# First attention of a six-layer kernel: the causal mask leaves TensorE and is added by GpSimd, and three steps are put in another order

## The reference

```python
scores = jnp.einsum('bhqd,bhkd->bhqk', qh, kh) * inv_sqrt_d
causal = jnp.tril(jnp.ones((sq, sk), dtype=bool))
scores = jnp.where(causal, scores, jnp.finfo(scores.dtype).min)
attn = jax.nn.softmax(scores, axis=-1)
out = jnp.einsum('bhqk,bhkd->bhqd', attn, vh)
return out.transpose(0, 2, 1, 3).reshape(b, sq, H) @ Wout.T      # x = x + this
```

## Time and profile before

| | |
|---|---|
| median of 3 runs | 1257.46 us (1254.38 to 1261.32) |
| the profiled execution | 1256.03 us |
| its span | 1254.2 us |
| busy in the span | PE 91%, PEld 70%, DVE 57%, ACT 35%, POOL 21% |
| mean granted clock of TensorE | 0.96 |

### The profile page before, as it was taken

How to read it: one execution, slowest core, us unless ns; L and a number is a source line. 1 busy time by engine, 2 the same in 40 slices (tenths; PEclk the granted TensorE clock), 3 DMA queues, 4 the chain that set the end, 5 groups by cost and what they waited for, 6 DMA issues and landing times. The chain is left out here.

```text
span 1254.2 us, 32458 instructions
## 1 busy us (share of the span) xinstructions
PE 1141.8 (91%) x12589; PEld 872.6 (70%) x12590; DVE 720.3 (57%) x1834; ACT 443.3 (35%) x1283; POOL 267.3 (21%) x343
## 2 busy tenths in 40 slices
PE   3899899999999889999969999999984887889997
PEld 1676688787887668987957777777754775546664
DVE  3788554455455465553257878888763998212221
ACT  0444353443343211211046555555521332112221
POOL 1600000000000000000144456445415220322222
PEclk9999899999999989999689999999996997899999
DMA  7521000000000076000002111111148112122221
GB/s 234 180 58 45 1 1 1 0 0 0 0 0 1 1 197 156 0 0 9 27 10 54 48 32 51 51 42 35 44 153 277 37 32 80 40 60 38 43 39 14
DMA packets 69644, 65.54 MB, mean 52 GB/s; under 512 B 32720, under 2 KB 60656, under 8 KB 68940
## 3 DMA queue, kind: packets, MB, share of 16 engines
q1 hardware_dynamic: 61612, 45.32, 14.0%
q0 software_dynamic: 7968, 19.32, 5.2%
HBM read 52.34 MB, written 13.19 MB: 52 GB/s over the span
## 5 line engine op out<-in xcount | busy, mean ns | idle before, releaser
L1532 ACT ACTIVATE xattn_exps<-xattn_ps_s,xattn_top 128x256 f32<-128x256 f32 x256 | 118.0, 475 | 77.5 <-DVE xattn_top L1600 77.5
L613 PEld LDWEIGHTS attn_ps_q<-attn_xnT,w_b_q 128*128 128x128 f32 x1024 | 118.8, 193 | 12.6 <-issue 12.6
L613 PE MATMUL attn_ps_q<-attn_xnT,w_b_q 128*128 128x128 f32 x1024 | 123.4, 276 | 0.0
L1099 POOL TENSOR_TENSOR fold_last_cos<-raw_last,all_consts 64x64 f32<-64x64 f32 x1 | 0.3, 314 | 538.3 <-POOLq L911 538.3
L667 PE MATMUL attn_ps_out<-w_b_o,attn_oT 128*128 128x256 f32 x480 | 106.5, 380 | 1.8 <-DVE all_x L848 1.5
L667 PEld LDWEIGHTS attn_ps_out<-w_b_o,attn_oT 128*128 128x128 f32 x480 | 90.0, 190 | 15.1 <-DVE all_x L848 2.4
L1607 DVE STREAM_TRANSPOSE xattn_expsT<-xattn_exps 128x1024 f32<-128x1024 f32 x64 | 79.5, 1242 | 22.6 <-ACT xattn_exps L1532 22.6
L721 ACT COPY attn_qT<-attn_ps_q 128x512 f32<-128x512 f32 x64 | 38.0, 594 | 148.2 <-PE attn_ps_q L613 148.2
L1597 DVE TENSOR_REDUCE xattn_raw_top<-xattn_ps_s 128x4 f32<-128x1024 f32 x64 | 77.8, 1216 | 13.6 <-PE xattn_ps_s L1424 13.3
L1424 PE MATMUL xattn_ps_s<-xattn_kT,xattn_qT 64*32 64x256 f32 x2048 | 69.6, 381 | 2.9 <-ACT xattn_exps L1532 2.9
L1434 PE MATMUL xattn_ps_o<-xattn_expsT,xattn_kv 32*64 32x256 f32 x2048 | 63.5, 380 | 4.6 <-DVE xattn_last_scores L1643 3.9
(11 more groups left out here) (325 smaller groups left out, 2309.2 us busy)
## 6 DMA issues: line engine op xcount, KB each, us to landing
xattn_inverse<-xattn_inverse_rows SPq DMA_DIRECT2D x30, 256.0 KB, 4.1
all_c<-in_ctx SPq DMA_DIRECT2D x64, 64.0 KB, 1.9
moe_gate<-in_f_gate SPq DMA_DIRECT2D x8, 512.0 KB, 8.6
moe_up<-in_f_up POOLq DMA_DIRECT2D x8, 512.0 KB, 7.2
moe_down<-in_f_down POOLq DMA_DIRECT2D x8, 512.0 KB, 12.9
sorted_x<-all_zeros SPq DMA_DIRECT2D x1, 2944.0 KB, 15.7
experts_x_in<-sorted_x SPq DMA_DIRECT2D x23, 128.0 KB, 2.3
xattn_v_stage<-xattn_v_rows SPq DMA_DIRECT2D x16, 136.0 KB, 1.8
```

Of the source, the lines that this page charges most:

```text
L613: last = nc.tensor.matmul(ps_q[g % 2][:, h * P:(h + 1) * P], wq[:, c, head * DH:(head + 1) * DH], xnT[u][:, c, :], start=(c == 0), stop=(c ...
L1532: nc.scalar.activation(exps[g % 2][:, nkeys * k:nkeys * (k + 1)], ps_s[g % 2][:, nkeys * k:nkeys * (k + 1)], ACT.Exp, bias=top[u][:, n:n + ...
```

## The change

In the first layer alone (`cross`):

- The two mask products per tile (L320) are dropped; the score products start their own accumulation.
- VectorE turns the 32 columns of the mask table once at the start (`causalT`), ahead of the roots of the first normalisation. Per tile, after VectorE has turned the scores (L506), GpSimd adds the turned mask, broadcast over heads, to them (128x512, f32, both inputs in SBUF) and writes `masked`; VectorE takes the maximum and the difference from `masked`.
- On VectorE, `softmax_head` is split. In step i the order becomes outs_ready(i-2), normalise(i+2), turn the scores of i, queries_out(i+1), then `softmax_rest(i)` (wait for GpSimd, maximum, difference), residual(i-2).
- On TensorE, turn_exps(i-1) moves from behind scores(i) to behind queries(i+1), directly ahead of finish(i-2); turn(i+2) moves behind weigh(i-1) and behind the waits of scores(i+1). On ScalarE, expsT_out(i-1) moves behind the copies of keys and values.
- `load_and_scale` becomes a generator: its first part (the loads for the second layer) runs first, then two scale operations after each of the first tiles' mask adds, and the loads `c_1` and `c_2` after that of tile 9.

```diff
-            if beside:
+            if cross:
+                work = beside(pool)
+                causal = causalT[:, :].unsqueeze(1).to_broadcast([P, HEADS, SEQ])
+                pool.wait_ge(causal_turned, 1)
+                next(work)
+                for t in range(TILES):
+                    pool.wait_ge(scores_out, t + 1)
+                    wait_count(pool, shifted_ready, t)
+                    nc.gpsimd.tensor_tensor(masked[:, :, :], scores_sb[:, :].rearrange("p (h k) -> p h k", h=HEADS), causal, ALU.add)\
+                      .then_inc(masked_ready, 1)
+                    if t < BESIDE_STEPS:
+                        next(work)
+            else:
                 beside(pool)
...
-            def scores(t):
+            def scores_waits(t):
                 pe.wait_ge(q_ready, t + 1)
                 pe.wait_ge(k_ready, t + 1)
                 wait_count(pe, scores_out, t)
-                for p in range(2):
-                    nc.tensor.matmul(ps_scores[:, 512 * p:512 * p + 256], ident16, causal16, start=True, stop=False, skip_group_check=True)
+
+            def scores(t):
+                if not cross or isinstance(t, int):
+                    scores_waits(t)
+                if not cross:
+                    for p in range(2):
+                        nc.tensor.matmul(ps_scores[:, 512 * p:512 * p + 256], ident16, causal16, start=True, stop=False, skip_group_check=True)
...
             def step(i, u, live):
                 if live(0):
                     scores(i)
-                if live(-1):
+                if not cross and live(-1):
                     turn_exps(i - 1)
                 if cross and live(-2):
                     turn_outs(i - 2, i + 2 if live(1) else TILES)
                 if live(1):
                     keys_values(i + 1, 1 - u)
                     queries(i + 1, 1 - u)
+                if cross and live(-1):
+                    turn_exps(i - 1)
                 if cross and live(-2):
                     finish(i - 2, i if live(-1) else TILES)
-                if live(2):
+                if not cross and live(2):
                     turn(i + 2)
                 if live(-1):
                     weigh(i - 1, 1 - u)
+                if cross and live(2):
+                    if live(1) and live(0):
+                        scores_waits(i + 1)
+                    turn(i + 2)
...
             if cross:
+                nc.vector.transpose(causalT[:, :], consts[:, C_CAUSAL:C_CAUSAL + SEQ]).then_inc(causal_turned, 1)
                 moments.roots(dve, dve_roots, EPS_LN)
...
             def softmax_head(t):
                 dve.wait_ge(scores_made, t + 1)
+                if cross:
+                    wait_count(dve, masked_ready, t)
                 for p in range(2):
                     last = nc.vector.transpose(scores_sb[:, p * 256:(p + 1) * 256], ps_scores[:, 512 * p:512 * p + 256])
                 last.then_inc(scores_out, 1)
-                dve.wait_ge(scores_out, t + 1)
+
+            def softmax_rest(t):
+                if cross:
+                    dve.wait_ge(masked_ready, t + 1)
+                    view = masked[:, :, :]
+                else:
+                    dve.wait_ge(scores_out, t + 1)
+                    view = scores_sb[:, :].rearrange("p (h k) -> p h k", h=HEADS)
                 s1.tile(t)
-                view = scores_sb[:, :].rearrange("p (h k) -> p h k", h=HEADS)
...
                 if live(0):
                     softmax_head(i)
+                    if not cross:
+                        softmax_rest(i)
                 if live(1):
                     if not cross:
                         values_out(i + 1, 1 - u)
                     queries_out(i + 1)
+                if cross and live(0):
+                    softmax_rest(i)
                 if live(-2) and cross:
                     residual(i - 2)
```

More of the change, by code:

```diff
@@ L26 @@
 MASKED = -1e30
+BESIDE_STEPS = 10
 C_IDENT = 0
@@ L217, in small_attention @@
     shifted = sb("shifted", [P, HEADS, SEQ])
+    masked = sb("masked", [P, HEADS, SEQ]) if cross else None
+    causalT = sb("causalT", [P, SEQ]) if cross else None
+    masked_ready, causal_turned = sem("masked_ready"), sem("causal_turned")
     exps = sb("exps", [P, HEADS * SEQ])
@@ L260, in _ @@
                 nc.gpsimd.memset(v_rows[u][:, :, :, HD], 1.0).then_inc(blank, 1)
-            if beside:
+            if cross:
[11 more added lines that the diff above has]
+            else:
                 beside(pool)
-            if not cross:
                 for t in range(TILES):
@@ L326, in scores @@
                             last = nc.tensor.matmul(ps_scores[rows, 512 * p + m * P:512 * p + (m + 1) * P], kT[half, m, rows],
-                                                    q_blocks[half, m, :, rows], start=False, stop=True, skip_group_check=True)
+                                                    q_blocks[half, m, :, rows], start=cross, stop=True, skip_group_check=True)
                 last.then_inc(scores_made, 1)
@@ L440, in step @@
                         values_out(i + 1, 1 - u)
+                if cross and live(-1):
+                    expsT_out(i - 1)
                 if live(0):
@@ L2112, in load_and_scale @@
             pool.dma_start(c_br[:, :], d["c_br"].partition_broadcast(P)).then_inc(got_c, 16)
+            yield
             for c in range(KC):
@@ L2116, in load_and_scale @@
                       .then_inc(b_scaled, 1)
+                    if n // SCALED % 2:
+                        yield
                 nc.gpsimd.tensor_scalar(b_kv[:, c, :], b_kv[:, c, :], b_g[:, c:c + 1], None, ALU.mult).then_inc(b_scaled, 1)
+            yield
             pool.dma_start(c_1[:, :, :], chunks(d["c_w1"])).then_inc(got_c, 16)
             pool.dma_start(c_2[:, :, :], chunks(d["c_w2"])).then_inc(got_c, 16)
+            yield
         phase = ExitStack()
```

## The result

The changed kernel takes 1274.53 us in the median of 4 runs (1273.60 to 1276.49), the kernel before 1259.01 us (4 runs, 1254.38 to 1261.32). The ratio is 1.0106, with a 95% interval of 1.0083 to 1.0130: slower by about 13 us by this ratio (the two medians lie 15.5 us apart), where +12.0 was forecast. The forecast was 1268.5 us with a range of 1263 to 1275, so the median lies just inside its upper edge. The profiled execution after took 1273.60 us, its span 1271.8 us.

The account below looks back on a forecast made before the run. VectorE's own 5.2 us per tile was taken as the bound, giving way to a 6.34 us chain: 13 steps 82.4 against 71.99, +10.4; with 0.2, 1.25 and 0.15, +12.0, forecast 1268.5 us, range 1263 to 1275.

Parts of the forecast that it names:

- the chain through VectorE: First layer: maximum and difference lengthen the closed TensorE-VectorE chain from 5.00 to 6.34 us per step; chance 0.70.
- VectorE's list is the bound before, so the mask products are worth 0: First layer: VectorE alone needs 5.2 us per tile, so freeing 0.31 us of TensorE per tile gains nothing.
- TensorE's order: finish waits for ScalarE's copy, about 0.85 us idle per step; TensorE's sum 5.8 us, covered by the 6.34 us chain.
- The add hidden up to about 2.1 us: GpSimd's mask add, taken as 1.46 us, costs nothing in a steady step up to about 2.1 us.
- The tail and the start: Last tile's bare add +1.25 us; tile 0's outputs +0.2; the mask turn ahead of the roots +0.15.
- The loads: Third layer's loads move to tile 9; the values' stall, 4.4 us, is gone; colliding again +4.4, 1273, chance 0.08.
- TensorE as the bound: Rival: the chain doesn't close and TensorE gets shorter, step 4.9 us, whole 1249.3; chance 0.05.
- GpSimd over its limit: Rival: GpSimd's add over 2.1 us, or its scale operations holding up the difference, whole 1274; chance 0.08.
- The clock: Rival: TensorE's clock falls in the new gaps, in half of the steps, +13, whole 1281; chance 0.03.
- The port rule: Shared VectorE-GpSimd port: the difference would wait up to 0.9 us in some ten steps; half of a 0.08 chance.

Follow-up runs that it names:

- x11: Kernel before with its old orders, no causal mask at all, loads spread as in the change and TensorE's wait for queries ahead of weigh: ratio 0.9971 to the kernel before.
- x1: Changed kernel with TensorE's and ScalarE's order of before: ratio 1.0113 to the kernel before.
- x3: Changed kernel without GpSimd's add, so the mask is left out: ratio 1.0125 to the kernel before.
- x8: x7 with the projection also in the free half of a scores bank: ratio 1.0046 to the kernel before.
- x2: Changed kernel with the projection written to the free half of a scores bank, every order kept: ratio 1.0169 to the kernel before.
- x6: Kernel before (mask products, VectorE's order, no add) with only TensorE's and ScalarE's new order and the loads spread: ratio 1.0103 to the kernel before.
- x7: Changed kernel with VectorE's maximum and difference moved a step later, ScalarE's exponential moved to match: ratio 1.0142 to the kernel before.
- x4: Changed kernel with the mask added twice on GpSimd: ratio 1.0187 to the kernel before.
- x5: Changed kernel with VectorE's maximum and difference back ahead of the masking of the queries: ratio 1.0179 to the kernel before.

## Why the prediction was right

The time lay in the range for the reason given, the chain through VectorE. Of the 6.0 us between the forecast of 1268.5 and the median of 1274.53 the first layer accounts for 1.5 (13.5 instead of 12.0). The forecast also started from 1256.5 us for the kernel before, which took 1259.01 in the median of four, 2.5 more; the remaining 2.0 us lie within the scatter of the other layers.

*VectorE's list is the bound before, so the mask products are worth 0.* Right: L320 is gone and nothing was gained. In x11, where they are simply left out, the step is no shorter than before.

*The chain through VectorE, 6.34 us.* Right as a mechanism, shown by x1 and x3: without TensorE's order, and without the add, the step stays 6.40 us and VectorE waits ahead of the queries. x8 against x2 shows it from the other side. It was sized 0.06 us short, 0.8 in 13 steps. The turned outputs to the last query product took 79.63 + 1.16 - 78.62 = 2.17 us and not 2.12, and I had taken the shorter of the two lengths that the stretch from L482 to the end of L486 alternates between. The first five steps took 6.5 each, 0.1 more than the others, 0.5 in all. Together +11.75 and not +10.4.

*TensorE's order: "the wait is covered by the chain. If that cover went, TensorE would set 5.8".* This is the step of the prediction that failed. The wait itself was right (0.77 us), its price without cover was not. I added it to TensorE's own list, and did not follow what waits for the instruction behind it: the projection feeds the residual, and the residual stands ahead of the outputs in VectorE's queue. x6 measures 6.35 us where the prediction said 5.8 and the expectation 6.0. It did no harm to the forecast because the other chain is as long (6.40), and two chains of nearly equal length cost no more than one. That was luck: nothing in the prediction compared the two, and a second chain 0.1 us longer would have set the step. It would have misled anyone who mended only the first (x7).

*The add hidden up to about 2.1 us.* Right, if a little short: in x4 the two adds, 2.6 us with their handover, stuck out by 0.3, so the limit is near 2.3. The add took 1.27 us, not 1.46. GpSimd's groups after:

```profile
L273 POOL TENSOR_TENSOR xattn_masked<-xattn_scores,xattn_causalT 128x512 f32<-128x512 f32 x16 | 20.3, 1271 | 57.7 <-DVE xattn_scores L537 57.7
```

VectorE's subtraction on as many elements takes 0.69 us. The Trainium skill, "GPSIMD Engine Reference", section "4.1 Engine selection", has GpSimd about twice as slow for two inputs; here it is 1.84 times.

*The tail and the start.* The end part took +1.66 us against 1.25 forecast, with the bare wait of 1.38 us where it was expected (131.83); the start took +0.09 against 0.35.

*The loads.* TensorE waited for the values once, 0.8 us, instead of 4.2: no collision at tile 9. This single wait was not forecast. The 4.4 us that I took out hold for the one trace I had read: the collision cost 0.4 us in the second trace of before, and the two differ by 2.3 us over the same 13 steps.

*The rivals.* TensorE as the bound: excluded by x11 and by the gaps. GpSimd over its limit: only in x4. The clock stayed at 1.00 in every steady stretch of the change though TensorE was busy for 81% of it. It did fall in other versions, once in x2's steady part and in the first steps of several, as x3 and x4.

The port rule didn't show on VectorE, but it did on GpSimd. In the change only one difference ran wholly beside a scale operation, and it took 0.710 us, the longest of the 16. The better test is x5, where eight of the 16 differences lay wholly beside the scaling. The durations of the difference in the change, of the difference in x5 and of the scale operations in x5 (ns minimum, median, maximum):

```profile
L551 DVE TENSOR_TENSOR xattn_shifted<-xattn_masked,xattn_top x16: 691/692/710, 38.8 to 132.6; 128x512 f32<-128x512 f32 x16
...
L551 DVE TENSOR_TENSOR xattn_shifted<-xattn_masked,xattn_top x16: 691/691/693, 37.9 to 138.4; 128x512 f32<-128x512 f32 x16
...
L2154 POOL TENSOR_SCALAR w_b_q<-w_b_q,w_b_g x16: 919/1078/1361, 37.2 to 87.0; 128x256 f32<-128x256 f32 x16
```

VectorE lost nothing. But a scale operation that began while the difference ran took 1.36 us, and the one just ahead of it 0.92 (pairs from 46.1, 52.2, 59.8, 73.0, 79.6 and 86.1 us). In the pair from 67.4 us it was the first that began beside the difference, and the first that took 1.36. Beside the maximum and the queries both of a pair took 0.92 (the change, from 80.9 us). The scaling has time to spare here, so the 0.44 us cost nothing; the prediction had weighed the rule for VectorE alone, and the cost fell on the other engine.

## What to carry to other kernels

When two engines' lists are both as long as the step, look for chains that close on themselves through both queues, and price a reordering by what it puts between two links of such a chain, even where the moved work is unchanged and the engine ends up with more idle time than before. Where no longer chain covers it (one did in the change, as x1 shows), a wait has the price of everything that is queued behind it and of everything that waits for that on other engines, which can be more than its engine's own list shows. And of two nearly equal chains, mending one shows nothing: x7 alone would have acquitted the chain that x8 shows to count.

## What the runs showed that I had not expected

The five untouched layers differ between profiled executions of the same kernel by 5.5 us in 1120, more than some effects asked about here; the step lengths inside the layer agree to 0.01 us (5.18 and 5.19 before; 6.40 in the change, x1 and x3). For a question about one stage, its own rows were a far finer measure than the whole time. The sum over 13 steps is coarser than the step, since a fall of the clock or a wait for the values moves single steps by 1 to 3 us, and even the mean of eight steps was caught once, in x2.
